# A pause after every fourth indirect transfer in two expert dispatches, and a third second-layer expert gathered by one-hot products

## The reference, cut to what matters

```python
x = x + L0_ffn(L0_cond(x, cond))     # attention, then 8 experts, 2 per token
x = x + L1_ffn(L1_cond(x, cond))     # a modulated linear map, then 8 experts, 2 per token

def L0_ffn(x):                       # three layers per expert, width 512
    _, idx = top_k(x @ expert_tokens.T, 2)
    return sum(mean(idx == e) * (gelu(gelu(x @ W1[e] + b1[e]) @ W2[e] + b2[e]) @ W3[e] + b3[e]))

def L1_ffn(x):                       # two layers per expert, width 512, capacity 320 rows
    probs = softmax(top-2 logits of x @ gate_w)
    rank  = running count of each expert over (choice, token); rows of rank >= 320 are dropped
    return sum(probs * (gelu(x @ c_fc[e] + fc_bias[e]) @ c_proj[e] + proj_bias[e]))
```

## Time and profile before

| | |
|---|---|
| median of three runs | 407.04 us |
| the profiled execution: its time / its span | 407.39 us / 405.6 us |
| PE busy | 298.0 us (73%) |
| DVE busy | 275.3 us (68%) |
| ACT busy | 183.6 us (45%) |
| POOL busy | 161.8 us (40%) |
| L687, the dispatches' transfers | 32, 31.6 us on POOL |
| L738, the last scatters | 24, 24.5 us on POOL |
| mean granted clock of TensorE | 0.869 of full speed |

### The profile page before, as it was taken

How to read it: one execution, slowest core, us unless ns; L and a number is a source line. 1 busy time by engine, 2 the same in 40 slices (tenths; PEclk the granted TensorE clock), 3 DMA queues, 4 the chain that set the end, 5 groups by cost and what they waited for, 6 DMA issues and landing times.

```text
span 405.6 us, 7518 instructions
## 1 busy us (share of the span) xinstructions
PE 298.0 (73%) x2367; PEld 183.2 (45%) x2367; DVE 275.3 (68%) x721; ACT 183.6 (45%) x406; POOL 161.8 (40%) x247
## 2 busy tenths in 40 slices
PE   3757689888988764568999999999609256767820
PEld 2454334433433232535666666666409133555720
DVE  3777978989976638568876787776484843755513
ACT  7441636767654534035545444444454006435602
POOL 8211257556523385711223542222310572074560
PEclk9956999999999985689999999999955685995985
DMA  5999199854300065150211782100030012220114
GB/s 165 335 222 262 69 287 262 270 151 113 110 32 3 2 173 190 46 144 13 79 29 35 234 251 71 26 21 15 20 112 0 33 52 67 54 71 27 32 36 155
DMA packets 23395, 43.28 MB, mean 107 GB/s; under 512 B 3693, under 2 KB 13644, under 8 KB 23358
## 3 DMA queue, kind: packets, MB, share of 16 engines
q0 software_dynamic: 8368, 26.47, 21.1%
q1 hardware_dynamic: 13758, 13.64, 12.9%
q10 hardware_dynamic: 1232, 2.70, 2.0%
HBM read 27.25 MB, written 15.30 MB: 105 GB/s over the span
## 4 chain that ended last, share of the span: by engine, by line
PE 46%; DVE 22%; issue 9%; DMA 6%; POOL 6%; ACT 5%; another core or an unknown queue 3%; SPq 1%; ACTq 1%; POOLq 0%; DVEq 0%
PE pair L1120 13%; DVE mA L1438 6%; PE bank L1245 4%; PE bank L1130 4%; PE bank L1141 3%; PE bank L1017 3%; PE pair L1108 3%; DVE w_sb L1377 2%; PE pair L976 2%; POOL x_slots L687 2%; POOL y_rows L738 2%; DMA back<-y_rows 2%; PE bank L1009 2%; PE pair L1233 2%
## 5 line engine op out<-in xcount | busy, mean ns | idle before, releaser
L1120 PE MATMUL pair<-w_sb,h 128*128 (+1 forms) x276 | 65.0, 386 | 2.3 <-DVE h L1561 2.3
L668 POOL TENSOR_SCALAR_AFFINE_SELECT p_ring<-p_ring 128x128 f32<-128x128 f32 (+2 forms) x88 | 40.3, 472 | 59.6 <-ACT p_ring L811 58.8
L811 ACT ACTIVATE p_ring<-bank 128x512 f32<-128x512 f32 (+1 forms) x88 | 44.5, 569 | 29.7 <-PE bank L996 29.5
L1438 DVE TENSOR_REDUCE mA<-pair 128x2 f32<-128x256 f32 (+3 forms) x64 | 50.3, 817 | 10.2 <-PE pair L978 10.1
L822 ACT ACTIVATE h<-pair,cols 128x128 f32<-128x128 f32 x92 | 26.3, 368 | 65.1 <-PE pair L1108 44.6
L722 POOL DMA_INDIRECT y_rows<-y_sb,id_now x21 | 24.2, 1154 | 68.1 <-DVE y_sb L1582 57.2
L687 POOL DMA_INDIRECT x_slots<-sent,slot x32 | 31.6, 986 | 32.8 <-DVE slot L1684 19.6
L1120 PEld LDWEIGHTS pair<-w_sb,h 128*128 128x128 f16 x276 | 26.0, 99 | 32.0 <-issue 4.6
L976 PE MATMUL pair<-kr,qr 128*128 128x128 bf16 (+3 forms) x128 | 33.5, 319 | 5.8 <-DVE mA L1438 4.6
L786 ACT ACTIVATE w_sb<-w_ring 128x1024 f16<-128x1024 f32 x24 | 25.4, 1059 | 25.5 <-DMA w_ring<-in_L_ffn_W_dram 25.5
L996 PE MATMUL bank<-qr,kr 128*128 128x512 bf16 (+3 forms) x128 | 29.9, 302 | 1.5 <-ACT p_ring L811 1.1
(11 more groups left out here) (290 smaller groups left out, 595.7 us busy)
## 6 DMA issues: line engine op xcount, KB each, us to landing
w_ring<-in_L_ffn_W_dram POOLq DMA_DIRECT2D x24, 512.0 KB
x_slots<-w_sb POOLq DMA_DIRECT2D x4, 1032.0 KB, 9.9
fc_sb<-in_L_ffn_c_fc_dram POOLq DMA_DIRECT2D x4, 512.0 KB
cp_sb<-in_L_ffn_c_proj_dram POOLq DMA_DIRECT2D x4, 512.0 KB
back<-y_rows SPq DMA_DIRECT2D x8, 256.0 KB, 3.3
kr<-k_rows SPq DMA_DIRECT2D x8, 204.0 KB
qr<-q_rows SPq DMA_DIRECT2D x8, 192.0 KB
x_slots<-w_sb ACTq DMA_DIRECT2D x1, 1290.0 KB, 6.7
```

The lines of the kernel that those rows point to most:

```text
L668: pool.affine_select(out=probs, in_=probs, compare_op=ALU.is_ge, fill=0.0, base=0, pattern=[[0, heads], [1, P]], channel_multiplier=-1).th ...
L811: act.activation(p_ring[:, w % P_RING, 0:width], bank(4 + v % 3)[:, 0:width], ACT.Exp).then_inc(exp_done, 1)
L1120: ins = mm(bank(3), h1[:, s, hq, k * P:(k + 1) * P], w2_sb[k][wq][:, bass.ds(e * HID, HID)], start=(k == 0 and n == 0), stop=(k == HC - 1 ...
L1438: dve.tensor_reduce(mA[:, b, t, g * G + 2 * hp:g * G + 2 * hp + 2], got[:, :, 0:(t + 1) * P], AX_X, ALU.max).then_inc(a_used, 1)
```

## The change

It has three parts. GpSimd waits, before the last four transfers of the first dispatch, until the first twelve have landed, and in the second dispatch before the third and the fourth group of four, until all that were issued before have landed. `EARLY` becomes 3, so expert 2 of the second layer is gathered by one-hot products, and its slots are loaded to `tg_early` for their row numbers only. In DVE's stream the row numbers of the early experts are made right after copy_t(e + 2) of the loop's first pass, ahead of split_h(e + 1) and add_bias(e).

```diff
-EARLY = 2
+EARLY = 3
...
             for k in range(2):
+                if k:
+                    pool.wait_ge(sent0, 16 * 3 * R)
                 dispatch(1, k, slot0, x0_d, sent0)
             load_weights(LAST_PAIR + 1)
...
                 if n < 2:
                     pool.wait_ge(xc_ready, 2 * (n + 1))
                     pool.wait_ge(slot1_ready, n + 1)
+                else:
+                    pool.wait_ge(sent1, 16 * R * n)
                 dispatch(b, k, slot1, x1_d, sent1)
...
             for e in range(EARLY - 1, E):
                 if e + 2 < E:
                     copy_t(e + 2)
-                if e + 1 < E:
-                    split_h(e + 1)
-                add_bias(e)
                 if e == EARLY - 1:
                     dve.wait_ge(early_in, 32 * EARLY)
                     for n in range(EARLY):
                         result_rows(n, tg_early[n].bitcast(I32)[:, :, D]).then_inc(id_ready, 1)
                         dve.wait_ge(id_ready, n + 1)
+                if e + 1 < E:
+                    split_h(e + 1)
+                add_bias(e)
```

## The result

The changed kernel took 401.74 us (median of four runs, 399.48 to 403.72), against 409.99 for four runs of the kernel before. The ratio is 0.9895, interval [0.9849, 0.9942], which is 1.05% less. Two further comparisons gave 0.9831 [0.9751, 0.9911] and 0.9829 [0.9765, 0.9893]. The forecast was 400.0 and 1.7% less (a ratio of 0.983, which lies outside the first interval and inside the two others).

The account below looks back on a forecast made before the run. No engine was taken as the bound: PE's signals reach others late while GpSimd issues transfers, then PE's experts and GpSimd's scatters follow. 407.39 - 2.0 - 5.0 = 400.4, given as 400.0 against 407.04; range 396 to 404, 8 in 10 within 393 to 410.

Parts of the forecast that it names:

- That PE's signals are late beside rows of transfers, and a pause lets them through: Both dispatches: PE's signals reach other engines late while GpSimd issues transfers; ACT's GELU of block 0 gains 4.1 at most.
- The first dispatch, -2.0: Wait before the first dispatch's last four transfers: between +1.1 and -4.1 us, taken as -2.0.
- The second dispatch's pauses, 2.2 us: Second dispatch: two pauses of 1.1 us each on GpSimd delay the last transfer by 2.2; SP's loads begin at 341.8.
- The third expert ... -5.0: Second layer: hidden(2) needs no load, so hidden(3) starts at about 348.3 instead of 353.34: -5.0 us, bounds +2.2 to -6.
- From hidden(3) on the order of work is the same: From hidden(3) to the end: project(3)'s slow 9.2 us beside the scatters stands, 0; could be -6 or about +3.
- The row numbers first ... I take nothing: DVE's row numbers before the scatters start near 349.3 instead of 354.14, -4.8, said to fit the -5.0; nothing counted.
- Only the third expert counts: Rival, 20%: the pauses free nothing and cost 1.1 and 2.2 us, hidden(2) saves its 2.48 idle: about 406 us.
- Slower: Rival, 15%: signals stay late, ACT copies the third gather before its first GELU, which starts after 339: 410.4 us.
- More is freed: Rival, 15%: signals on time everywhere and the slow project(3) shrinks too: -4, -6 and -4 to -6, 393 to 396 us.
- The marks beside the transfers, 0.5 us: Second dispatch: DVE's eight added marks hold GpSimd's transfers, 0.24 us each for two, 0.5 us, inside a 1 us allowance.

Follow-up runs that it names:

- T: The kernel before with only the third expert gathered by products (EARLY = 3), no waits, old order of the row numbers: 413.48 us, ratio 1.0167.
- R: The kernel before with only the early experts' row numbers moved ahead of split_h and add_bias, no waits, two early experts: 404.22 us, ratio 0.9911.
- e5: The changed kernel without the second dispatch's two waits, the first dispatch's wait kept: 408.8 us, ratio 1.0063.
- W alone: The kernel before with only GpSimd's three waits added, two early experts and the old order of the row numbers: 408.36 us, ratio 1.0007.
- W and T: The changed kernel with the early experts' row numbers made after split_h and add_bias, as before: 407.52 us, ratio 1.0011.

## Why the prediction was right or wrong

**The size: near, and by luck.** 400.0 was forecast; the profiled execution took 399.82, the median of the four runs was 401.74, and the 1.7% came out as 1.05% in the first measurement and as 1.7% in the two others. But the sum's larger term was put on the wrong part, and its chances with it: the forecast rested on T, which alone costs 1.7%, and gave nothing to R, which alone gains 0.9%.

**That PE's signals are late beside rows of transfers, and a pause lets them through: right.** In the changed kernel the delays of the earlier trace rows shrink from 4.7 to 0.1 us and from 7.4 to 3.4. With one wait in the second dispatch the latter is 3.5, with memsets 4.8, and without any wait there it is 10.4 (e5). That freed signals shorten the time is another matter: W alone gains nothing.

**The first dispatch, -2.0: right in its stage** (1.9 shorter by the profiles), open in the time. The loads of blocks were to land in time if block 0 came no more than some 3 us earlier. The text held that DVE's list runs without a hole up to 182.75, which would cap the gain; the earlier trace rows show one of 3.66 us before 171.12, and the copy of 182.75 came 3.5 us earlier, counted from the first transfer (34.77 to 31.23). Counted so, ACT's GELU came 4.3 us earlier (174.06 - 147.98 before, 171.42 - 149.59 after), and PE then waits 4.40 us for the loads (181.72).

**The second dispatch's pauses, 2.2 us: somewhat too small.** The transfers after the pauses start 2.56 and 3.33 us after the ones before them, where the spacing is 1.3: 3.3 us in both. SP's loads began 2.7 us after the last transfer (341.44 - 338.76). The 341.44 for the forecast 341.8 is luck of the clock: counted from d1 they began at 26.1, where the forecast has 25.3.

**"The third expert ... -5.0": the step that failed.** hidden(3) did come 5.3 us earlier from d1 (36.8 to 31.5; 32.8 and 32.0 in the two other profiles), as worked out. That this carries to the end is what the runs refute: W and T has hidden(3) at 31.9 and a ratio of 1.0011. The wrong step is "From hidden(3) on the order of work is the same", with the slow stretch beside the scatters let stand at 0. Measured, PE's way from hidden(3) to its last product takes 34.4 us before, 39.3 in W and T, 28.0 in R alone, and 33.0, 35.9 and 36.1 in the three profiles of the change. The prediction had named both directions (-6, or some 3 more with nine ready) and counted neither.

**"The row numbers first ... I take nothing": the term that was left out.** The text had their start 4.8 us earlier and remarked that it fits the -5.0, and then counted the other one. Counted from d1, the first scatter moved from 38.95 to 34.7, 36.0 and 35.3 in the three profiles, 3.6 in the mean. R alone gains 0.9%, with its first scatter 3.3 us earlier (38.95 - 35.6), its hidden(3) 2.3 us later, and PE's last product 4.0 us earlier. So a gain belonged to this term; whether by the earlier start or by the breaks in the row of scatters stays open, and the chain of R alone passes through DVE's operations on the experts there, not through the first scatter.

**The rivals.** "Only the third expert counts" (406) fell: the pauses do free the signals, and the third expert alone takes 413.48. "Slower" had the mechanism of T alone right, in its place: ACT must copy the third gather before its first GELU, which then starts at 339.07, past the 339 that was named. It put the price at 410.4; without the waits it is dearer (1.0167), and with the row numbers a pass later too (with R added it is 1.0063). In the changed kernel the waits keep it from happening. "More is freed" was not needed: one unnamed piece of 2.71 us is left.

**The marks beside the transfers, 0.5 us.** Under the Trainium skill, "SBUF — State Buffer", section "SBUF: two separate sides", DVE's added marks would hold GpSimd's transfers if they run in a two-port mode; no view shows the mode. In the trace they held none: the marks from 328.39 to 330.25 have transfers of 0.96 and 0.99 us beside them (328.40 and 329.67). Others did grow. All instructions of the tile `x_slots`, against the earlier trace rows (min, median, max in ns):

```profile
L687 POOL DMA_INDIRECT x_slots<-sent,slot x32: 954/964/1722, 149.6 to 338.8; - x32
...
DMA to landing us min/median/max: 2.1/3.4/11.3
```

The longest, 1722 ns at 330.96, has no mark beside it. What the Trainium skill says on the same page under "Who interferes with whom" (PE and ACT never wait for another engine's access) leaves the late signals unexplained, as the prediction said; what carries them no run shows.

## What to carry to other kernels

Before giving a milestone's gain to the total, follow it through the stage behind: here PE's 5 us were lost again in its own products beside a row of scatters. Then look at what the first instruction of the last queue waits for: a few small DVE operations (0.16 us each) stood ahead of 24 scatters, and moving them in the list was the only part that gained alone. Where a change has several parts, run each alone and in pairs: one part cost 1.7%, one gave nothing and repaired the first, one gave 0.9%, and the sum looked like the forecast. Between rows of indirect transfers from GpSimd a break after four lets late signals through, but that is worth something only if the engine so freed doesn't then wait for the data of the same transfers.

## What was not expected of the hardware

Signals of PE came up to 8.7 us late beside unbroken transfers (in R alone the first half of hidden(0) ended at 330.95, and ACT's GELU of it began at 339.69, "remote"), and a pause of 1.35 us, in which GpSimd ran five memsets, was enough to let them through. The end of the row is not always the moment of release: in R alone the last transfer's instruction had ended at 337.15 (336.20 + 0.95), 2.5 us before that GELU. Beside unbroken scatters PE's own products also stood, with no wait that the profile names, for up to 1.9 us at a time (8.3 us in all in W and T; 0.4 in the first 20 us of scatters in R alone and 2.2 in all, where they come in rows of three and six). And the stretch from the first scatter to the end stayed within 47.4 to 51.8 us over twenty profiles, though PE's standing in it differed by 8 us; why these balance stays open.
